# A mixture of experts after attention: every expert on every token, against rows sorted by expert through DRAM

## The reference

```python
x = x + deformable_conv(group_norm(x))            # conv stage, the change leaves its arithmetic alone
t = tokens(x)                                     # 8 images x 256 tokens x 64
n = layer_norm(t)
q, k, v = n @ Wq.T + bq, n @ Wk.T + bk, n @ Wv.T + bv
t = t + softmax(q @ k.T / 8) @ v                  # within an image
n = layer_norm(t)
probs = softmax(n @ gate_w + gate_b)              # 16 experts
top, idx = top_k(probs, 2); top /= sum(top)
dispatch = zeros(16); dispatch[idx] = top
h = silu(n @ w1[e]) * (n @ w2[e])                 # 64 -> 128, every expert e
t = t + sum_e dispatch[e] * (h @ w3[e])           # 128 -> 64
```

## Time and profile before

| what | us |
|---|---|
| three runs | 456.14, 458.97, 459.05; median 458.97 |
| span of the profiled execution, first to last instruction | 457.2 |
| conv stage | 0 to 257.2 |
| token stage | 257.2 to 457.2 |
| PE, DVE, ACT, POOL busy | 410.0, 335.2, 259.5, 141.3 |

### The profile page before, as it was taken

The page is one execution under the profiler, slowest core; times in us unless marked ns, Lnnn a source line. Parts: engine busy times, 40 slices in busy tenths (PEclk is TensorE's granted clock), DMA queues, the critical chain, the costliest instruction groups (busy, mean ns, idle before and its releaser), DMA issues. The chain is left out here.

```text
span 457.2 us, 9731 instructions
## 1 busy us (share of the span) xinstructions
PE 410.0 (90%) x3276; PEld 232.0 (51%) x3276; DVE 335.2 (73%) x730; ACT 259.5 (57%) x571; POOL 141.3 (31%) x172
## 2 busy tenths in 40 slices
PE   1689999999999999999998457989999999999995
PEld 0543343433534335343332345867677776767663
DVE  3479967789777897777889346768777686868652
ACT  2683645746457464574610154676767677685752
POOL 2263223243232422324200164123242333324322
PEclk9979999999999999999999655799999999999997
DMA  8068886938559385583860330000000000000000
GB/s 258 3 155 218 215 222 148 229 89 227 163 122 231 91 226 158 117 239 86 226 162 1 141 134 0 2 0 2 2 0 14 3 0 14 1 2 1 11 3 11
DMA packets 28409, 44.91 MB, mean 98 GB/s; under 512 B 6864, under 2 KB 11088, under 8 KB 27984
## 3 DMA queue, kind: packets, MB, share of 16 engines
q1 hardware_dynamic: 28368, 44.39, 37.6%
HBM read 6.11 MB, written 0.52 MB: 15 GB/s over the span
## 5 line engine op out<-in xcount | busy, mean ns | idle before, releaser
L663 DVE TENSOR_TENSOR prod<-ps_t,a_rep 128x1024 f32<-128x1024 f32 x128 | 152.0, 1219 | 34.5 <-PE ps_t L363 32.3
L363 PE MATMUL ps_t<-b,vt 32*128 32x512 f32 x512 | 74.7, 650 | 1.9 <-DVE prod L663 1.9
L769 POOL TENSOR_TENSOR a<-a,mask 128x512 f32<-128x512 f32 (+1 forms) x40 | 47.0, 1178 | 83.7 <-ACT a L523 81.4
L383 PE MATMUL ps_d<-prod,keep 128*32 128x512 f32 x512 | 69.0, 611 | 0.3 <-DVE prod L663 0.2
L1223 POOL TENSOR_TENSOR total<-total,share 128x256 f32<-128x256 f32 x56 | 40.9, 730 | 86.9 <-DVE share L1117 86.5
L304 PEld LDWEIGHTS ps_m<-om_r,sel 128*128 128x128 f32 x193 | 29.0, 187 | 75.3 <-ACT mask L501 28.2
L1101 DVE TENSOR_TENSOR hidden<-ps_h,gated 128x256 f32<-128x256 f32 x128 | 51.4, 415 | 3.7 <-ACT gated L1316 2.8
L1316 ACT ACTIVATE gated<-ps_h 128x256 f32<-128x256 f32 x128 | 47.8, 387 | 7.5 <-PE ps_h L1436 1.1
L304 PE MATMUL ps_m<-om_r,sel 128*128 128x256 f32 x193 | 49.3, 334 | 0.0
L1117 DVE TENSOR_TENSOR share<-ps_yf,factor 128x256 f32<-128x256 f32 x56 | 23.7, 423 | 30.4 <-issue 12.8
L1310 ACT ACTIVATE factor<-ps_yf 128x256 f32<-128x256 f32 x64 | 24.6, 385 | 37.3 <-PE ps_yf L1471 37.3
(11 more groups left out here) (151 smaller groups left out, 671.3 us busy)
## 6 DMA issues: line engine op xcount, KB each, us to landing
a_rep<-a SPq DMA_DIRECT2D x128, 256.0 KB, 4.7
a_rep<-a SPq DMA_DIRECT2D x32, 128.0 KB, 2.8
w_f<-in_w SPq DMA_DIRECT2D x2, 1024.0 KB, 5.8
start<-in_start SPq DMA_DIRECT2D x1, 1344.0 KB, 7.8
x_turned<-in_x_turned SPq DMA_DIRECT2D x1, 512.0 KB, 3.8
t_tok<-in_x SPq DMA_DIRECT2D x1, 512.0 KB, 9.4
w<-in_w SPq DMA_DIRECT2D x1, 512.0 KB, 7.6
select_f<-in_select SPq DMA_DIRECT2D x1, 512.0 KB, 8.4
```

What stands on the lines that cost most here:

```text
L363: mm = pe.matmul(out, vt[par][r, v % 2, :, :, :].rearrange("p j y c -> p (j y c)"), b[par][r, pair_taps(v // 2), :].rearrange("p t x -> p ...
L383: mm = pe.matmul(ps_d[r, :], fold[:, v % 2, :], p, start=v == 0, stop=False, skip_group_check=True)
L663: dve.tensor_tensor(p[:, :, :], t[:, :, :], a_rep[par][:, ms, pair_taps(v // 2), :].rearrange("p m t x -> p m (t x)"), ALU.mult).then_inc( ...
L769: pool.tensor_tensor(v, v, mask[(PAIRS * par + k) % 2][:, 0:wide, :], ALU.mult).then_inc(a_done, 1)
```

## The change

The token stage is written anew. The parts, with the names in the diff:

- **Attention on couples.** Two images at once, 4 couples in `COUPLES + 2` = 6 rounds. No operand is split any more: the products are plain float32. Both images lie side by side on the partitions, so `q_w` and the others are block-diagonal. `scores` are 4 products of 64 rows by 256 columns, `project_qkv` 2 of 256 columns and 4 of 128, `turn_p` 8 transposes, `values` 8 products. DVE and ACT take the same steps as before on twice the tokens.
- **Ranking.** For each couple DVE finds the two largest logits and their indices; PE (`rank`) counts by matrix products how many earlier tokens chose the same expert. The result is a row number for each token and choice, in a region of 2048 rows for every expert in DRAM.
- **Placing.** POOL (`place`) writes each token's normed row, share and return address (66 numbers, 264 bytes) to its two rows with 8 indirect DMAs a couple, 32 in all.
- **Tiles.** From the counts DVE makes a table of 47 steps, each with an expert and a first row. A step takes 128 rows; 47 is the most that can be needed, and all 47 are run. SP loads both numbers of a step into registers and starts three DMAs (the expert's weights, and the rows twice). PE turns, multiplies, ACT and DVE make the hidden layer, PE multiplies by `w3`, ACT scales by the share, and POOL scatters the result by the return address with one indirect DMA (`send`). Buffers go round in a ring of 6.
- **Sum.** When all 47 are sent, SP loads both parts of every token, DVE adds them, SP stores.
- **Blanks.** The rows in DRAM are first filled with ones, 8.65 MB, by 8 DMAs of 1.08 MB and a small one on SP's queue in the conv stage, in between the fills. POOL clears the source tile.
- Gone: the splitting, the dispatch product, the 128 products of expert and image, the weights held in SBUF.

```diff
+            def blank_slots(first, last):
+                view = slots[0:DEAD, :].rearrange("(p r) c -> p (r c)", p=P).rearrange("p (j a b) -> p j a b", a=2, b=BLANK)
+                for j in range(first, last):
+                    sp.dma_start(view[:, j, :, :], spread(blank[:, :], 1, 2)).then_inc(blank_in, 16)
...
+            sp.wait_ge(blanked, 1)
+            blank_slots(0, 3)
             fill(0, 0)
+            blank_slots(3, 5)
             fill(1, 1)
+            blank_slots(5, 8)
+            sp.dma_start(slots[DEAD:DEAD + P, :], blank[:, 0:ROW]).then_inc(blank_in, 16)
...
 @block.sync
+            for s in range(STEPS):
+                b = s % RING
+                if s == 0:
+                    sp.wait_ge(tab_done, 1)
+                    sp.wait_ge(placed, 16 * 2 * TT)
+                expert_row = sp.value_load(table[1:2, s:s + 1], min_val=0, max_val=(EXPERTS - 1) * P)
+                if positive(s - RING + 1):
+                    sp.wait_ge(y_ps, s - RING + 1)
+                sp.dma_start(w_in[b][:, :], w_rows[bass.ds(expert_row, P), :]).then_inc(w_here[b], 16)
+                row = sp.value_load(table[0:1, s:s + 1], min_val=0, max_val=DEAD)
+                if positive(s - RING + 1):
+                    sp.wait_ge(sent[b], 16 * (uses(s) - 1))
+                sp.dma_start(x_in[b][:, 0:C], rows[bass.ds(row, P), 0:C]).then_inc(x_here[b], 16)
+                sp.dma_start(x_in[b][:, C:C + ROW], rows[bass.ds(row, P), :]).then_inc(x_here[b], 16)
...
+            for q in range(COUPLES):
+                sp.dma_start(both[q][:, :, :, :], parts_view[:, K * q:K * (q + 1), :, :]).then_inc(both_in[q], 16)
...
 @block.gpsimd
+            def place(q):
+                pool.wait_ge(ln_done[1], q + 1)
+                for i in two:
+                    k = K * q + TPI * i
+                    pool.tensor_copy(stage[:, k:k + TPI, :, 0:C], spread(normed[1][:, :, i, :], 2, 2)).then_inc(staged, 1)
+                pool.wait_ge(staged, 2 * (q + 1))
+                pool.wait_ge(blank_in, 16 * BLANKS)
+                pool.wait_ge(slot_done, q + 1)
+                pool.wait_ge(share_done, q + 1)
+                for k in range(K * q, K * (q + 1)):
+                    for w in two:
+                        pool.indirect_dma_start(
+                            out=rows[:, :], out_offset=bass.IndirectOffsetOnAxis(ap=slot_at[:, k, w:w + 1], axis=0),
+                            in_=stage[:, k, w, :], in_offset=None, bounds_check=DEAD - 1, oob_is_err=False)\
+                            .then_inc(placed, 16)
+            def send(s):
+                b = s % RING
+                pool.wait_ge(y_done, s + 1)
+                pool.indirect_dma_start(
+                    out=parts[:, :],
+                    out_offset=bass.IndirectOffsetOnAxis(ap=x_in[b][:, C + ROW - 1:C + ROW].bitcast(I32), axis=0),
+                    in_=y_sb[b][:, :], in_offset=None, bounds_check=2 * TT * P - 1, oob_is_err=False)\
+                    .then_inc(sent[b], 16)
+            for r in range(ROUNDS):
+                project, attend, gate = stages(r)
+                if gate is not None:
+                    power(1, gate)
+                if project is not None:
+                    power(0, project)
+                if gate is not None:
+                    place(gate)
+            for s in range(STEPS):
+                send(s)
...
 @block.tensor
+            for s in range(STEPS):
+                if s + 2 < STEPS:
+                    turn_in(s + 2)
+                if s + 1 < STEPS:
+                    products(s + 1)
+                output(s)
```

More of the change, by code:

```diff
@@ L864, in token_stage @@
[L864 to L872, removed]
@@ L884, in token_stage @@
[L884 to L894, removed]
+        ident, ones, q_bias, k_bias = at["ident"], at["ones"], at["q_bias"], at["k_bias"]
+        minus_half = sb("minus_half2", [P, K])
@@ new lines, in token_stage @@
+        hots = sb("hots", [P, K, EXPERTS])
+        tally = sb("tally", [P, COUPLES, EXPERTS])
+        pick = sb("pick", [P, K, 2, EXPERTS])
+        slot_f = sb("slot_f", [P, K, 2])
+        slot_at = sb("slot_at", [P, TT, 2], I32)
+        stage = sb("stage", [P, TT, 2, ROW])
+        full = sb("full", [P, EXPERTS], I32)
+        tiles = sb("tiles", [P, EXPERTS], I32)
+        flat = sb("flat", [P, EXPERTS])
+        ends = sb("ends", [P, EXPERTS])
+        skip = sb("skip", [P, EXPERTS])
+        past = sb("past", [P, EXPERTS])
@@ new lines, in token_stage @@
+        skipped = sb("skipped", [P, EXPERTS])
+        sums = sb("sums", [P, 2])
+        cols = sb("cols", [P, 2])
+        table = sb("table", [2, P], I32)
+        x_in = [sb(f"x_in{b}", [P, C + ROW]) for b in range(RING)]
+        w_in = [sb(f"w_in{b}", [P, HIDDEN + C]) for b in range(RING)]
+        xs = [sb(f"xs{b}", [P, P]) for b in two]
+        gated = [sb(f"gated{b}", [P, P]) for b in two]
+        hidden = [sb(f"hidden{b}", [P, P]) for b in two]
+        y_sb = [sb(f"y_sb{b}", [P, C]) for b in range(RING)]
@@ new lines, in invert_sums, with add_values @@
+            def invert_sums(q):
+                dve.wait_ge(o_ps, q + 1)
+                dve.reciprocal(rsum[:, :], ps_o[:, :, C]).then_inc(rsum_done, 1)
+            def add_values(q):
+                dve.wait_ge(rsum_done, q + 1)
+                for k in range(K):
+                    tokens = t_tok[:, K * q + k, :]
+                    op = dve.scalar_tensor_tensor(out=tokens, in0=ps_o[:, k, 0:C], scalar=rsum[:, k:k + 1], in1=tokens,
+                                                  op0=ALU.mult, op1=ALU.add)
+                op.then_inc(res_done, 1)
@@ L1196, in _ @@
+            step_table()
+            keep_x(0)
+            keep_x(1)
+            hide(0)
+            for s in range(STEPS):
+                if s + 2 < STEPS:
+                    keep_x(s + 2)
+                if s + 1 < STEPS:
+                    hide(s + 1)
+            for q in range(COUPLES):
+                finish(q)
         @block.gpsimd
@@ L1231, in _ @@
-            for r in range(ROUNDS):
-                project, attend, gate, serve = stages(r)
-                for slot in range(SLOTS):
-                    p = duet_at(r, slot)
-                    if p is not None and p >= 2:
-                        add(p - 2)
-                    if slot == 0 and gate is not None:
-                        power(1, gate)
-                    if slot == 0 and project is not None:
-                        power(0, project)
-                    if slot == 1 and gate is not None:
-                        keep_x(gate)
-                    if piece_at(r, slot) is not None:
-                        low_piece(piece_at(r, slot))
@@ new lines, in gap_exps, with silu @@
+            def gap_exps(q):
+                act.wait_ge(gap_done, q + 1)
+                if positive(q):
+                    act.wait_ge(share_done, q)
+                act.activation(gap_exp[:, :], gap[:, :], ACT.Exp).then_inc(gap_expd, 1)
+            def silu(s):
+                act.wait_ge(h_ps, s + 1)
+                if positive(s - 1):
+                    act.wait_ge(hidden_done, s - 1)
+                act.activation(gated[s % 2][:, :], ps_h1[s % 2], ACT.Silu).then_inc(silu_done, 1)
@@ new lines, in shared @@
+            def shared(s):
+                b = s % RING
+                act.wait_ge(y_ps, s + 1)
+                if positive(s - RING + 1):
+                    act.wait_ge(sent[b], 16 * (uses(s) - 1))
+                act.activation(y_sb[b][:, :], ps_y[s % 2], ACT.Copy, scale=x_in[b][:, C + ROW - 2:C + ROW - 1])\
+                   .then_inc(y_done, 1)
+            for r in range(ROUNDS):
+                project, attend, gate = stages(r)
+                if attend is not None:
+                    exps(attend, 0)
+                if gate is not None:
+                    turned(1, gate)
+                if attend is not None:
+                    exps(attend, 1)
+                if project is not None:
+                    turned(0, project)
+                if attend is not None:
+                    copy_p(attend, 0)
+                    copy_p(attend, 1)
+                if gate is not None:
+                    gap_exps(gate)
+                if project is not None:
+                    qkv(project)
@@ L1352, in _ @@
+            silu(0)
+            for s in range(STEPS):
+                if s + 1 < STEPS:
+                    silu(s + 1)
+                shared(s)
         @block.tensor
@@ L1516, in _, with turn_p @@
-            output(DUETS * IMAGES - 1)
-            turn_sum(IMAGES - 1)
+            def turn_p(q):
+                for i in two:
+                    pe.wait_ge(exp_done, K * q + TPI * (i + 1))
+                    if positive(2 * (q - 1) + i + 1):
+                        pe.wait_ge(p_done, 2 * (q - 1) + i + 1)
+                    for t in range(TPI):
+                        for k in range(TPI):
```

(70 more changed lines are left out.)

886 lines of the change are left out of this document (348 added, 538 removed).

## The result

| | before | after |
|---|---|---|
| median of the runs | 458.66 us (456.14 to 459.05, 4 runs) | 532.86 us (531.87 to 533.84, 4 runs) |
| ratio, 95% interval | | 1.163, 1.159 to 1.167: slower |
| profiled span | 457.2 us | 530.1 us |
| PE busy | 410.0 us, 90% | 373.8 us, 71% |

The account below looks back on a forecast made before the run. PE was taken to bound the token stage before; afterwards attention without cover, then steps at SP's pace. 257.2 + 8 + 124.1 + 111.9 + 8.0 + 8.9 = 518.1 us of span, forecast 520, range 450 to 565.

Parts of the forecast that it names:

- conv stage with the blanks: Conv stage: 257.2 us plus 8 for blanks on SP's queue delaying copies of later images, ends 0 and 12.
- attention until SP starts: Token stage: attention on couples without cover, scatters on the path and a landing, 124.1 us until SP may start.
- 32 scatters: POOL's queue in attention: all 32 scatters lie on the path at 1.2 us each, 38.4 us.
- 47 steps: Tile stage: SP's three issues and two register loads bound each step at 2.38 us, 111.9 us in all.
- last step, loads, sum, store: After SP's last issue: 8.0 us for the last step, then 8.9 for loads, sum and store.
- A conv stage still ending at 257: Sign of a wrong prediction, at the conv stage's end; the right sign was an end near 265.
- the reckoning: SP's address work with each register load in a step: load and reckoning together 0.5 us, against 0.42 for another SP instruction.
- The ring: Six buffers of the tile stage: each held 8.0 us, so 1.3 us a step, under SP's 2.38 and not the bound.
- rival (a): Tile steps: register loads cost next to nothing, a step is PE's 1.4 to 1.5 us; 42 less, 478; chance 0.22.
- (b): Issue cheap on both queues: POOL's scatter costs 0.42 us, SP as in rival (a); 451 us, faster; chance 0.15.
- (c): Tile steps: landings of small rows take 7.6 us, so the ring gives 3.2 a step; 40 more, 560; chance 0.13.
- (d): Tile stage: the change does not skip as it says; all 47 steps run whatever the counts, already in the sum.

Follow-up runs that it names:

- the kernel whose copies came 0.8 us late: The kernel after with the 47 addresses written in as constants instead of register loads, and a ring of 12 buffers instead of 6: 480.78 us.
- the lean kernel: The kernel after with register loads kept, but without range tests, and finished addresses in the table, so no multiplication on SP: 505.31 us.
- the constant addresses: The kernel after with the 47 addresses written in as constants instead of SP's register loads, ring still 6: 491.87 us.
- the last kernel: The kernel after with scatters behind the next round's `power`, lean loads, weights from ACT's queue and a ring of 12: 449.52 us median, 0.981 of before.

## Why the prediction was right

The place of the loss and its sign were as forecast: attention without cover, then 47 steps at SP's pace. The size came within 12 us of span, partly by luck: 8.3 too much on the blanks stand against 20.2 too little on the rest. The sum against the trace:

| term | forecast, us | measured, us |
|---|---|---|
| conv stage with the blanks | 257.2 + 8 | 256.9 |
| attention until SP starts | 124.1 | 126.6 |
| of it 32 scatters | 38.4 | 40.1 |
| 47 steps | 111.9 | 127.5 |
| last step, loads, sum, store | 16.9 | 19.0 |
| span | 518.1 | 530.1 |

**The blanks** were mis-sized: 8 us, ends 0 and 12, and the lower end came. A conv stage still ending at 257 stood among the prediction's own signs of being wrong. DVE's first weights of images 1 and 2 stood at 58.98 and 88.44, against 58.08 and 88.05. The step that failed is the price of the blanks, 218 to 258 GB/s, the rate of the copies and of the loads. Windows of before, then of after: the same stretch; a part of it in which nearly all bytes are blanks; a stretch of copies alone:

```profile
45.70:57.00 11.30, 11.26 (x91) 4.38 (x83) 11.20 (x14) 7.29 (x16) 3.28 (x3) 1.00 0.90 217
45.70:57.00 11.30, 11.26 (x87) 4.51 (x87) 11.19 (x13) 7.25 (x16) 3.29 (x3) 1.00 0.98 300
47.70:52.50 4.80, 4.80 (x38) 1.68 (x31) 4.80 (x6) 3.69 (x8) 2.00 (x2) 1.00 1.03 400
55.00:66.00 11.00, 10.94 (x208) 5.58 (x204) 8.76 (x10) 6.61 (x13) 2.82 (x3) 1.00 0.90 220
```

The reason given, that DMA at 87% leaves little to catch up with, held: the share rose from 0.90 to 0.98 only. But at a full share the blanks, in pieces of 4224 bytes, moved 400 GB/s, where the copies, in pieces of 2048, move 220 at 0.90. Why the rates differ so is not shown. At 400 GB/s the two blanks before image 1 take 5.4 us and not 8.4 to 9.9, the three before image 2 8.1 and not 12.6 to 14.9 (estimates from that window). The first two copies had landed at 57.30 for image 1 (51.44 before) and at 87.61 for image 2 (76.81 before), each just in time for the weights, where the prediction had 97 to 99 for image 2.

That blanks in front of the copies can hold DVE up, the doubled blanks (+21 us) show; the kernel whose copies came 0.8 us late (+4.9) fits it.

**Attention** came within 2.5 us, by errors that cancel. The first two rounds took 21.2 us, not 25.3: scores took 1.6 us in the first round, not 3.6, since the products on the two halves of the rows run beside each other (two at a time start 0.01 apart), and the clock was higher than the 0.50 that I kept. Windows of the first two rounds together, of the fourth, and of the fifth:

```profile
256.90:278.20 21.30, 13.73 (x68) 10.88 (x68) 6.54 (x34) 5.54 (x14) 2.35 (x6) 0.76 0.00 0
306.80:322.00 15.20, 10.28 (x64) 9.01 (x64) 7.63 (x45) 3.68 (x10) 2.78 (x5) 0.75 0.01 2
332.00:348.60 16.60, 10.17 (x44) 9.18 (x44) 6.32 (x41) 2.41 (x6) 1.82 (x4) 0.50 0.01 3
```

The third and fourth took 18.4 and 15.2 against 19.4 and 16.1. The fifth and sixth took 16.6 and 12.6 against 12.9 and 10.0, for which the prediction shows no working (16.1 without the projection's 3.7 is 12.4). The clock had fallen to 0.50 for good by then, but the forecast had reckoned with 0.50; two of its terms were too small at that clock. `values` was put at 1.9, the time of one image's 4 products (8 instructions, 1.97), and a couple has 8 (16 instructions): they took 3.43 in the fifth round at clock 0.50, and 1.80 in the third only because the clock was 1.00 from 291.0 to 293.3. The ranking, put at 1.4, took 3.0 in the fifth round (338.68 to 341.72). The scatters are on the path as forecast, 8 in 10.1 us, 1.28 from one to the next where I took 1.2.

**The steps** were SP-bound as forecast, with the largest error of the sum, 15.6 us. Of the 2.68 the three issues with their gaps have 1.24 (forecast 1.38), and each load with its reckoning 0.72, not 0.5. The mis-sized term is the reckoning: 0.27 for the load is less than the 0.42 taken for it, but the 0.08 left for the reckoning is 0.44 in the trace, of which the range tests, not counted at all, and the multiplication make 0.28. With the cheaper issues that is 0.3 a step, 14 us; the steps that take 3.0 and more make the rest. The Trainium skill (DMA: Bandwidth & Descriptors, Latency and other measured facts) gives about 600 ns as the floor of such a load; here the load occupies SP for 0.27, and 0.47 pass from one issue to the next with a load between them in the lean kernel, so the floor doesn't hold on this queue. The 121.3 that it gave for the steps was nearer to the 127.5 than mine, but by luck: the load was cheaper than the floor, and register work made up for it.

**The ring** was not the bound, as forecast, but by less than I thought: 1.3 a step was wrong. PE turns the rows of step s + 2 before it puts out step s, so a buffer is held for two more steps. With a hold of h plus two steps and six buffers a step is h / 4; the forecast's h = 8.0 gives 2.0, and 1.91 was measured. It would have been the bound for rival (a): with SP cheap I put 478, and the constant addresses gave 492. Only with the larger ring did it come to 481.

**The rivals.** (b) is out, since a scatter keeps POOL for 0.97 and the next follows 0.30 later. Its sum takes 44 from (a) where (a) has 42, so 453 and not 451, which changes no chance. (c) is out too: the rows land in 1.8 us and the scatters of results in 2.4 (medians of the DMA issues), and SP waits for neither within the steps. (d), that all 47 steps run, holds; the counts of these inputs need 42.

What stays open: why the clock stays at 0.50 with PE busy for 30 of 30 us in the steps, when the rounds before, at 20.1 of 21.0, had 1.00. No kernel here tried it. Only in part explained is why the step was 2.15 with the weights on ACT's queue, bound by the same ring that gave 1.91 with constant addresses: the later `y_sb` adds 0.51 to the hold, which by h / 4 is 0.13 of the 0.24.

## What to carry to other kernels

Skipping work moves the bound to whoever finds out what to skip: here 128 products at full clock gave way to 47 small steps, paced by the queue that turns table entries into addresses, so count the register instructions around a dynamic address, not the load alone. When a step waits for nobody, relieve it and read the next wait: SP, ring and PE stood at 2.68, 1.91 and 1.55, and each had to be moved for the next to pay. An issue that takes an engine's time belongs in its queue behind whatever the critical path wants from that engine next: moving 24 scatters behind one small instruction was worth 27 us.

## What the runs showed of the hardware

- A scatter of 128 rows by indirect DMA keeps POOL for 0.97 us, and the next starts 1.28 after the start of the first, whether the rows have 264 or 256 bytes; it lands 2.2 to 2.4 us after its issue.
- A register load on SP takes 0.27 us, and the register work behind it 0.44; without the two range tests and the multiplication of the address it is 0.16.
- A DMA share says how long the engines were busy, not what they moved: SP's queue moved 400 GB/s at a share of 1.03 with the blanks (pieces of 4224 bytes) and 220 at 0.90 with the copies (2048 bytes).
- TensorE's granted clock stayed at 0.50 (1.2 GHz) over 72 us in which PE was busy for 68.7 with small float32 products (the steps of the last kernel).
